# A two-layer graph network kernel with its batch loops written out in full

## The reference, cut to what matters

```python
# layer 0, 4 heads of 64, softmax over chunks of 256 neighbours
scores = clip(einsum('bhnd,bhjcd->bhnjc', q, kc) / sqrt(Dh), -10, 10)
scores = where(mask == 0, -10, scores)
attn = softmax(scores, axis=-1)
ctx = einsum('bhnjc,bhjcd->bhnd', attn, vc)
out = layernorm(ctx @ Wo.T + bo + x) * gamma + beta
x = layernorm(x + out)
# layer 1
Wh = h @ W; s_i = Wh @ a1; s_j = Wh @ a2
e = leaky_relu(s_i[:, :, None] + s_j[:, None, :], 0.2)
attention = softmax(where(adj > 0 or i == j, e, -inf), axis=-1)
x = layernorm(x + elu(attention @ Wh))
```

## Time and profile before

| | us |
|---|---|
| timed runs, median of 3 (lowest, highest) | 3712.26 (3709.11, 3714.05) |
| the profiled execution, whole | 3715.06 |
| its span, first to last instruction | 3713.2 |
| TensorE busy in the span | 3538.6 (95%) |
| VectorE busy | 2930.0 (79%) |
| ScalarE busy | 2545.3 (69%) |
| GpSimd busy | 2244.2 (60%) |

### The profile page before, as it was taken

How to read it: one execution, slowest core, us unless ns; L and a number is a source line. 1 busy time by engine, 2 the same in 40 slices (tenths; PEclk the granted TensorE clock), 3 DMA queues, 4 the chain that set the end, 5 groups by cost and what they waited for, 6 DMA issues and landing times. The chain is left out here.

```text
span 3713.2 us, 135473 instructions
## 1 busy us (share of the span) xinstructions
PE 3538.6 (95%) x57302; PEld 2495.4 (67%) x57302; DVE 2930.0 (79%) x3447; ACT 2545.3 (69%) x3746; POOL 2244.2 (60%) x1152
## 2 busy tenths in 40 slices
PE   5999999999999999999999999996599999999998
PEld 2656766665665676567566666653478888888886
DVE  6687787678678767767867876885699999999986
ACT  2666666666666666656666666664488889898887
POOL 1797788688778878878977887896021212212220
PEclk9999999999999999999999999997799999999999
DMA  6010010001001000100100100001122122122211
GB/s 231 3 37 15 20 37 14 15 21 43 15 14 37 20 15 21 36 14 15 43 14 20 37 20 14 14 20 47 46 58 69 47 81 69 58 69 69 58 35 57
DMA packets 128571, 145.48 MB, mean 39 GB/s; under 512 B 29777, under 2 KB 113617, under 8 KB 125905
## 3 DMA queue, kind: packets, MB, share of 16 engines
q1 hardware_dynamic: 126704, 136.14, 11.4%
q10 hardware_dynamic: 1248, 0.40, 0.1%
HBM read 102.70 MB, written 33.75 MB: 37 GB/s over the span
## 5 line engine op out<-in xcount | busy, mean ns | idle before, releaser
L403 ACT ACTIVATE probs<-probs 128x1024 f32<-128x1024 f32 x1024 | 1083.6, 1058 | 768.0 <-DVE probs L865 747.0
L281 POOL TENSOR_TENSOR psums<-probs 128x1024 f32<-128x1024 f32 x512 | 1253.1, 2448 | 462.6 <-ACT probs L403 461.5
L515 PE MATMUL ctx_ps<-probs,v_rows 64*32 64x512 f32 x16256 | 1475.8, 590 | 7.1 <-DVE seg_ctx L802 5.3
L865 DVE SCALAR_TENSOR_TENSOR probs<-sc_ps,edges 128x1024 f32<-128x1024 f32 x1024 | 1226.1, 1218 | 311.7 <-PE sc_ps L502 301.6
L502 PE MATMUL sc_ps<-q_cols,k_cols 64*32 64x512 f32 x16384 | 1200.6, 590 | 22.1 <-DVE probs L865 21.7
L1414 PE MATMUL out_ps<-wh,e 128*128 128x257 f32 x4096 | 927.6, 382 | 50.8 <-DVE e L1541 48.6
L1414 PEld LDWEIGHTS out_ps<-wh,e 128*128 128x128 f32 x4096 | 773.9, 191 | 170.3 <-issue 40.7
L515 PEld LDWEIGHTS ctx_ps<-probs,v_rows 64*32 64x32 f32 x16256 | 665.0, 106 | 279.5 <-issue 182.6
L502 PEld LDWEIGHTS sc_ps<-q_cols,k_cols 64*32 64x32 f32 x16384 | 549.2, 107 | 298.0 <-issue 176.0
L509 PE MATMUL den_ps<-psums,ones 64*32 64x512 f32 x4064 | 600.1, 591 | 13.9 <-DVE seg_ctx L802 7.9
L305 POOL TENSOR_TENSOR ctx_t<-ctx_t,seg_ctx 128x1024 f32<-128x1024 f32 x224 | 545.0, 2433 | 52.3 <-DVE seg_ctx L802 52.1
(11 more groups left out here) (96 smaller groups left out, 3181.4 us busy)
## 6 DMA issues: line engine op xcount, KB each, us to landing
x_cols<-in_xT SPq DMA_DIRECT2D x8, 2048.0 KB, 7.9
probs<-in_adjT SPq DMA_DIRECT2D x16, 1024.0 KB, 8.6
x_rows<-in_x SPq DMA_DIRECT2D x32, 512.0 KB, 3.9
x<-res SPq DMA_DIRECT2D x32, 512.0 KB, 2.9
x_in<-x SPq DMA_DIRECT2D x32, 512.0 KB, 4.4
x_res<-x SPq DMA_DIRECT2D x32, 512.0 KB, 4.8
out<-h SPq DMA_DIRECT2D x32, 512.0 KB, 3.2
high<-rows SPq DMA_DIRECT2D x16, 512.0 KB, 4.1
```

Of the source, the lines that this page charges most:

```text
L281: pool.tensor_tensor(psums[:, q % 2, pair, :], probs[:, (SJ * q) % RING, pair, :], probs[:, (SJ * q + 1) % RING, pair, :], ALU.add).then_i ...
L403: act.activation(probs[:, n % RING, pair, :], probs[:, n % RING, pair, :], ACT.Exp, scale=DH ** -0.5).then_inc(s_exp, 1)
L515: return pe.matmul(ctx_ps[quad(h), z, :], v_rows[head_rows(r), n % JB, at:at + QUAD], probs[head_rows(r), n % RING, h, :], start=start, st ...
L865: dve.scalar_tensor_tensor(out=probs[:, n % RING, pair, :], in0=sc_ps[:, p, :, :], scalar=-LIM, in1=clip_hi[:, j, c * CW:(c + 1) * CW][:, ...
```

## The change

Both `Fori` loops become Python loops. Every pass is written out, `i` is a number everywhere, and so every wait is for a constant and every address is fixed. The order of the instructions of each engine, their tiles and their semaphores stay as they are. Register operations and branches are no longer in the program; it has three copies of what was one loop body.

```diff
--- before.py
+++ after.py
@@ -103,7 +103,7 @@
         for c in range(2):
             chunk((0, 0), c, c, True)
         one = ((0, 2), (0, 3), (1, 0), (1, 1))
-        with engine.Fori(0, B // 2 - 1) as i:
+        for i in range(B // 2 - 1):
             for s, c in one + tuple((s + 1, c) for s, c in one):
                 chunk((i, s), c, 2, True)
         i = B // 2 - 1
```

## The result

| | before | changed |
|---|---|---|
| timed runs, median (lowest, highest), us | 3710.69 (3708.66, 3714.05) | 3676.94 (3675.93, 3688.9) |
| the profiled execution, us | 3715.06 | 3676.80 |
| its span, us | 3713.2 | 3675.0 |

The ratio of the timed runs is 0.9914, 95% interval 0.99 to 0.9928. A later set of runs of both kernels gave 3677.75 against 3712.9, ratio 0.9902 (0.988 to 0.9924).

A forecast was written before the change was run, and what follows sets the result against it. TensorE, busy 95% of the span, was taken to bound the kernel. 3713.2 - 38.9 (layer 0) - 2.1 (layer 1's edges) = 3672.2 us of span, plus 1.86 outside it: 3674.1 us; range 3665 to 3704.

The forecast's parts named there:

- blocked addition: Layer 0: VectorE's addition of x (L835) losing further handovers to GpSimd; 4.9 us each, one or two giving 3679 to 3684.
- part 2: The loops' taken branches go: 1.07 us each in layer 1, 2.1 for both; layer 0's counted within the 38.87 us.
- Part 1: Layer 0: register arithmetic goes, each loop batch becomes like the written-out one behind the loop, 308.66 us; gain 38.87 us.
- The division of the 38.87 us: Layer 0's gain split: 29.1 us steady difference, 9.8 us disturbances (one blocked addition 4.9, two back edges with echoes 4.9).
- the 6.32 us case: Layer 0: longest L835, at 1086.37, outlasting two more GpSimd instructions; claimed to disagree with the skill's one-instruction port lock.
- Part 3: Whole program: more instructions, each to be fetched, but inferred to be fetched every pass already; cost 0.
- B: Rival, layer 0: registers don't set the phase, chunk patterns lock as in the loop; gain only 11.9 us, 3703; chance 0.14.
- C: Rival, layer 0: the shift holds in chunk 2 alone or every other batch; 3689 us (3684 to 3697); chance 0.07.
- E: Rival, layer 0: slower, new phase makes L835 lose handovers, two a batch; +18 us, 3731; chance 0.04.
- D: Rival, whole kernel: nothing changes measurably, edges hidden by TensorE's queue; 3705 to 3720 us; chance 0.05.

## Why the prediction was right

**The forecast and its terms.** 3674.1 was forecast and 3676.9 measured; the execution profiled has 3675.0 of span where 3672.2 was forecast. Layer 0's six batches take 2068.48 - 211.78 = 1856.7 us in place of 1890.8: 34.1 us less, where 38.9 were forecast. The missing 4.8 are the blocked addition (312.42 against 308.66 is 3.8 of them) and 1.0 net in the five others. It was priced at 4.9 as a case inside the forecast. That the sum is only 2.8 off is partly luck: layer 1 gave 2.1 us that no term had (part 2), which hid nearly half of layer 0's miss.

**Part 1.** The bound by the traced whole held nearly: the written-out stretch of 308.66 us stood for six that average 309.45. Its cause was argued from three instances of L835. In the whole trace of before 60 of the 64 instances, and 56 in that of the changed kernel, end 0.55 us (within 0.02) behind the GpSimd instruction that they met, and the experiments show what follows from it. Take away the two instructions that read two tiles, and the loop's batch is short with all its registers; load the sequencers without registers, and the written-out batch is long, unless the two instructions are gone. Of the 33.0 us that the six batches gain between TensorE's marks, 24.0 are there only with the two instructions (33.0 - 9.0). That part is phase, and the register operations are one of the things that set it. Of the other 9.0, 7.9 go when the edges are fetched early, and 1.1 are left for the registers.
The division of the 38.87 us was misread, though the sum doesn't depend on it. The two stretches taken as undisturbed, 313.51 and 313.56 us, each hold a taken branch of TensorE near their end (at 829.4 and 1461.5), and their marks fell 52 and 92 TensorE instructions short of a batch's 6666; so 307.75 and 307.61 us busy weren't the same work. In equal work the steady difference is 314.1 - 308.7 = 5.4 us a batch, 32 in all and not 29.1; the two edges are 2.1 us each, and the blocked addition was worth 1.7 there, not 4.9. In the changed kernel it was worth 4.1.
What the argument had too simple is that it counts L835 alone. The sum also holds L828, and GpSimd's own instructions grow (255 against 249 us a batch). And what the prediction cites of the Trainium skill ("SBUF — State Buffer", "SBUF: two separate sides") doesn't say which engine goes next when the port comes free. So the 6.32 us case, three GpSimd instructions one behind the other, isn't against it, though the prediction says so.

**Part 2.** The edges of layer 1 were worth 1.07 us each at the marks, and all are gone: 69.47 us between marks. Layer 1 is 4.2 us shorter in all (1130.5 to 1126.3 from its first transfer to the end), not 2.1. The other 2.1 fall ahead of its first product of L1414, at TensorE's lower clock (last section), and the forecast had no term for them; whether they belong to the change stays open. In layer 0 the edges were sized by a remainder, 4.9 with their echoes for both: 4.2 at TensorE's marks, and 7.9 in the kernels without the two instructions.

**Part 3.** Straight code costs nothing that these rows show: less instruction traffic, and PE waits 1.0 to 1.5 us in the batches without a long addition.

**The rivals.** B (the pattern locks where the loop has it) is out: no batch is at 313.5 with L835 at 13.6. Its evidence, that two loop stretches repeat within 0.1 us, was chance, since they hold 6614 and 6574 TensorE instructions. Something of it was true in another form: a small steady load, as in the kernel with increments, keeps the long form for the whole run. C's time, 3684 to 3697, is about that of the kernel in which TensorE alone keeps its loop (3697.2), but not its pattern, since there all batches are of middle length. E has one blocked addition, at 3.8 to 4.1 us where 4.9 were priced. D is out by the interval.

**What was too narrow.** "The new stretches contain none" was said of blocked additions from one stretch. The changed kernel had a blocked addition in one of two profiled executions, and one timed run of 3688.9 us that wasn't profiled. And TensorE's loop isn't harmless: the kernel that leaves only TensorE in its loop kept half of the loss.

## What to carry to other kernels

Where VectorE instructions with two SBUF inputs run beside a busy GpSimd, compare their lengths in two stretches of the same work before anything else. Here one instruction ranged from 0.7 to 6.3 us with the GpSimd instructions that it met, and through it register operations or bare increments moved the whole kernel by 0.6%. Cut such stretches on the engine that bounds the kernel, and compare the instruction counts of the windows: a mark on another engine slides, and a disturbance then shows in the wrong stretch. A stretch that is already written out behind a loop is a cheap measurement of what unrolling brings. And judge such a change by several profiled executions, since the same program took 3674.6 to 3688.9 us, with a blocked addition in one profile and none in the other.

## What the runs showed of the hardware that was not expected

A blocked addition passes over GpSimd instructions that had not begun when it was issued: it was issued during L281 (ending at 594.08), and the next two started 0.06 and 0.07 us ahead of their predecessor's end and went first. The Trainium skill ("SBUF — State Buffer", "SBUF: two separate sides") describes one holder for one instruction and doesn't say who is next. Here the waiting engine lost two handovers in a row, six times in the ten profiled executions of kernels with L835.

TensorE's taken branches took 3.4 to 5.1 us in these kernels, and 0.44 to 0.76 when the start of the loop was asked for in advance.

TensorE's granted clock at the start of layer 1, windows of 2 us (busy times of PE, PEld, DVE, ACT, POOL; the clock is the number ahead of the DMA's two), in before and then in the changed kernel:

```profile
2596.67:2598.67 2.00, 2.00 (x6) 1.52 (x6) 0.17 (x1) 0.39 (x1) 0.00 (x0) 0.50 0.54 190
2598.67:2600.67 2.00, 2.00 (x9) 1.66 (x8) 1.20 (x2) 0.45 (x2) 0.00 (x0) 0.75 0.00 0
```

```profile
2556.68:2558.68 2.00, 2.00 (x10) 1.68 (x10) 0.00 (x0) 0.77 (x2) 0.00 (x0) 0.50 0.06 23
2558.68:2560.68 2.00, 1.39 (x10) 1.25 (x8) 0.22 (x1) 1.51 (x3) 0.26 (x1) 0.82 0.42 122
2560.68:2562.68 2.00, 1.39 (x6) 1.24 (x7) 0.34 (x2) 0.20 (x1) 0.30 (x1) 1.00 0.83 252
```

TensorE had idled before both, between the layers, and both begin at half clock, 1.2 GHz. Their first products start 7.8 and 7.9 us behind the layer's first transfer (2582.67 and 2548.68). Before stays at half clock until about 17 us behind that transfer, the changed kernel until about 11, with the same instructions in the same order. Between the two, sixteen products of L1383 take 5.67 us in before and 3.77 in the changed kernel, most of the 2.1 us that layer 1's preparation lost or won. Of the first ten kernels profiled, the five in which no layer is written out on all engines have the late form (first product of L1414 69.4 to 69.8 us behind the transfer) and the five others the early one (67.1 to 67.7), which would make it part of the change. But the loop kernel with early-fetched edges and without the two additions has the early form too (66.3), with both loops in place. The cause stays open.
